# A dynamic 3x3 conv block: far and near parts in place of stacked rows, and fp32 products on two 64x128 tiles

## What is computed

```python
f = relu(einsum('oc,nchw->nohw', Wc, x) + bc)            # 64 channels
gk1 = relu(mean(x, (2, 3)) @ Wc.T + bc)
g_kern = (gk1[:, :, None] * Wkk + bkk).reshape(N, 64, 3, 3)
xm = x.reshape(N, 256, 3, 16, 3, 16).max(axis=(3, 5))
sk = relu(einsum('oc,nckl->nokl', Wc, xm) + bc)
gs = stack([g_kern, sk], axis=2)
dynW = relu(einsum('oj,ncjkl->nockl', Wck, gs) + bck)   # a 3x3 kernel per image and channel pair
y = conv3x3(f, dynW, pad=1) + b_ad                      # each image with its own weights
out = einsum('oc,nchw->nohw', Wf, y) + bf               # back to 256 channels
return x + out
```

## Time and profile before

| | us |
|---|---|
| median of 3 runs | 511.19 (509.42 to 512.63) |
| span of the profiled execution | 507.5 |
| PE busy | 487.8 (96%) |
| ACT busy | 426.6 (84%) |
| DVE busy | 418.9 (83%) |
| POOL busy | 296.2 (58%) |

### The profile page before, as it was taken

How to read it: one execution, slowest core, us unless ns; L and a number is a source line. 1 busy time by engine, 2 the same in 40 slices (tenths; PEclk the granted TensorE clock), 3 DMA queues, 4 the chain that set the end, 5 groups by cost and what they waited for, 6 DMA issues and landing times.

```text
span 507.5 us, 19231 instructions
## 1 busy us (share of the span) xinstructions
PE 487.8 (96%) x8349; PEld 383.7 (76%) x8349; DVE 418.9 (83%) x653; ACT 426.6 (84%) x486; POOL 296.2 (58%) x231
## 2 busy tenths in 40 slices
PE   5989999999999999999999999999999999999993
PEld 2454664677788888888888978888887878888781
DVE  6978879988888889888888988888889887888544
ACT  5779999998999999999999899999999989995231
POOL 5224586555577655556775555577655556765543
PEclk9999999999999999999999999999999999999997
DMA  8945778999898998998999999989999998953467
GB/s 335 418 134 201 265 283 289 366 353 349 323 333 334 323 332 340 348 359 293 320 362 333 333 365 343 318 297 360 307 366 334 341 333 298 361 208 145 185 270 296
DMA packets 48868, 158.01 MB, mean 311 GB/s; under 512 B 4752, under 2 KB 15888, under 8 KB 48784
## 3 DMA queue, kind: packets, MB, share of 16 engines
q1 hardware_dynamic: 34096, 93.07, 54.0%
q10 hardware_dynamic: 14688, 63.70, 31.0%
HBM read 75.94 MB, written 75.50 MB: 298 GB/s over the span
## 4 chain that ended last, share of the span: by engine, by line
PE 81%; ACT 2%; DVE 0%; issue 0%; DVEq 0%; ACTq 0%
PE ps L1129 30%; PE ps L1260 23%; PE ps L1228 21%; PE ps L1179 7%; ACT unused L609 1%; DVE X L859 0%; ACT unused L596 0%; ACT f_hi L688 0%; DVEq L153 0%; ACT f L694 0%; ACT Y L586 0%; PE ps L1372 0%; ACT dyn_b L709 0%; ACT dyn_hi L707 0%; ACTq L130 0%
## 5 line engine op out<-in xcount | busy, mean ns | idle before, releaser
L859 DVE SCALAR_TENSOR_TENSOR X<-ps,out_bias,X 128x960 f32<-128x960 f32 (+1 forms) x189 | 185.2, 1008 | 17.1 <-PE ps L1260 16.8
L1260 PE MATMUL ps<-Y,const 64*64 64x480 f32 (+1 forms) x1536 | 165.1, 486 | 0.0
L596 ACT ACTIVATE unused<-X,neg_mean 128x2304 bf16<-128x2304 f32 x60 | 132.0, 2201 | 0.4 <-DVE neg_mean L998 0.4
L512 POOL TENSOR_TENSOR dyn_a<-const,pool_g 128x576 f32<-128x576 f32 x30 | 34.9, 1165 | 163.8 <-DVE pool_g L883 163.8
L609 ACT ACTIVATE unused<-X 128x2304 bf16<-128x2304 f32 x60 | 126.9, 2115 | 0.0
L1228 PE MATMUL ps<-X,wcn_t 64*64 64x384 f32 (+1 forms) x1296 | 115.5, 486 | 0.7 <-issue 0.7
L935 DVE TENSOR_REDUCE feats<-X 128x6 f32<-128x1536 f32 x64 | 111.6, 1744 | 0.0
L1228 PEld LDWEIGHTS ps<-X,wcn_t 64*64 64x64 f32 x1296 | 82.0, 133 | 29.8 <-issue 7.4
L1260 PEld LDWEIGHTS ps<-Y,const 64*64 64x64 f32 x1536 | 78.2, 133 | 7.5 <-issue 2.8
L527 POOL TENSOR_TENSOR f_lo<-f,f_hi 128x1152 f16<-128x1152 f32 x32 | 71.4, 2232 | 19.5 <-ACT f L694 19.5
L1129 PE MATMUL ps<-f_hi,dyn_hi 64*64 64x480 f16 x1152 | 69.0, 365 | 2.5 <-ACT dyn_hi L715 1.1
(11 more groups left out here) (101 smaller groups left out, 541.8 us busy)
## 6 DMA issues: line engine op xcount, KB each, us to landing
X<-x SPq DMA_DIRECT2D x63, 1152.0 KB, 9.5
out<-X ACTq DMA_DIRECT2D x54, 1152.0 KB, 9.7
out<-X SPq DMA_DIRECT2D x7, 1152.0 KB, 8.0
out<-X SPq DMA_DIRECT2D x6, 480.0 KB, 3.5
stack<-f_hi SPq DMA_DIRECT2D x64, 32.5 KB, 2.5
stack<-f_lo SPq DMA_DIRECT2D x64, 32.5 KB, 5.4
X<-x SPq DMA_DIRECT2D x2, 576.0 KB, 7.1
upper<-f_hi SPq DMA_DIRECT2D x32, 32.5 KB, 3.5
```

Source lines behind the costliest of these rows:

```text
L596: nc.scalar.activation(unused[:, t], pixels(u, t), ACT.Square, scale=1.0 / SIDE, bias=neg_mean[:, n % 2, 1:2], accum_out=feats[:, (n + 1) ...
L859: nc.vector.scalar_tensor_tensor(out=out, in0=unit_psum(piece, bank, col), scalar=out_bias[:, t:t + 1], in1=out, op0=ALU.add, op1=ALU.add) ...
L1260: mm = nc.tensor.matmul(ps[rows, bank + q, col:col + width], wft[lanes, t, rows], Y[lanes, n % 2, at:at + width], start=True, stop=True)
```

## The change

The conv has a far and a near part in place of a main and a rest part. Each is made in three terms of nine taps on four 64x64 tiles, from f alone: 7 rows (336 columns) a tile for the far part, in banks 0 and 1, and 5 rows (240 columns) for the near part, in columns 256 on of banks 4 and 5, which the projection and the statistics also use. The tiles `stack` and `upper` and their DMAs are gone; four small DMAs an image bring the one row of f_hi and f_lo on each side of the seam. ACT copies both parts to Y, of which there is one. The projection uses three chunks of 512, 512 and 128 columns on 128x64 tiles throughout. A unit of the far part is two fp32 products of 336 columns on 64x128 tiles, made in one bank pair; the two near units are made in two turns of 240 columns. Units 1, 2, 3 and 5 use banks 6 and 7, units 0 and 4 banks 2 and 3. POOL takes the high weights and the relu from ACT and the Newton steps of the normalisation from DVE; ACT takes the gains. All stores are issued by SP. All orders are new. The core of the diff:

```diff
-CONV_BANKS = (0, 1)
-REST_BANK = 6
+ROWS = (7, 5)
+PART = tuple(rows * SIDE for rows in ROWS)
+FIRST = (((0, 7), (10, 17)), ((14, 19), (0, 5)))
+NEAR_BANK = 4
+NEAR_AT = 256
+CHUNKS = ((0, 512), (512, 512), (1024, 128))
+UNIT_BANKS = (2, 6, 6, 6, 2, 6)
...
@@ PE @@
-            def product(n, k, t, piece, bank, col):
-                at, width, _ = PIECES[piece]
-                for q, h in ((0, 0), (1, 1), (0, 1), (1, 0)):
-                    lanes, rows = (slice(CM * tile, CM * (tile + 1)) for tile in (q, h))
-                    mm = nc.tensor.matmul(ps[rows, bank + q, col:col + width], wft[lanes, t, rows],
-                                          Y[lanes, n % 2, at:at + width],
+            def product(n, k):
+                t, piece = OUT_UNITS[k]
+                at, width = PIECES[piece]
+                bank = unit_bank(n, k)
+                for h in range(2):
+                    lanes = slice(CM * h, CM * (h + 1))
+                    mm = nc.tensor.matmul(ps[:, bank + h, 0:width], wft[lanes, t, :], Y[lanes, at:at + width],
...
+            def conv(n, part, term):
...
+                if term == 0:
+                    pe.wait_ge(f_evac, count(n, 1, 2))
+                    pe.wait_ge(dyn_hi_ready, highs_done(n, 0))
+                    wait(pe, y_done[part], n)
+                    if part == NEAR:
+
+                        pe.wait_ge(halo_hi[n % 2], 32 * (n // 2 + 1))
+                        pe.wait_ge(f_evac, count(min(n + 2, N), 0, 2))
...
+            def units_near(n):
+                if not inside(n):
+                    return
+                pe.wait_ge(y_done[NEAR], count(n, 1))
+                wait_left(pe, n, 0)
+                pe.wait_ge(f_evac, count(min(n + 3, N), 0, 2))
+                wait_left(pe, n, 3)
+                products_near(n)
...
             for i in range(1, N - 1):
-                conv_main(0, i)
...
+                conv(i, FAR, 0)
+                unit(1, i - 1)
+                if i > TURN:
+                    project_f(i + 1)
+                    unit(2, i - 1)
+                    conv(i, FAR, 1)
+                    group_sums(i + 2)
+                    unit(3, i - 1)
+                    conv(i, FAR, 2)
...
+                units_near(i - 1)
+                conv(i, NEAR, 0)
+                conv(i, NEAR, 2 if i < SUMS else 1)
+                conv(i, NEAR, 1 if i < SUMS else 2)
+                unit(0, i)
...
@@ DVE @@
             for i in range(TURN + 1, N - 1):
-                unit(3, i - 2)
                 middle_maxima(0, i + 2)
-                unit(0, i - 1)
+                unit(1, i - 1)
                 outer_maxima(0, i + 2)
-                gains(i + 1)
                 middle_maxima(1, i + 2)
-                unit(1, i - 1)
-                outer_maxima(1, i + 2)
-                unit(4, i - 1)
-                unit(5, i - 1)
                 unit(2, i - 1)
                 variance(i + 2)
                 negate_mean(i + 3)
-                y_rest_out(i)
-                normalise(i + 2)
+                outer_maxima(1, i + 2)
+                unit(3, i - 1)
+                invert(i + 2)
+                unit(4, i - 1)
+                unit(5, i - 1)
+                unit(0, i)
...
@@ ACT @@
+            for i in range(TURN + 1, N):
+                y_out(i - 1, NEAR)
                 features(i + 1)
+                channel_mean(0, i + 3)
+                channel_mean(1, i + 3)
+                f_out(i + 1)
+                deviation(i + 2)
+                square_sum(0, i + 3)
+                y_out(i, FAR)
+                square_sum(1, i + 3)
...
@@ POOL @@
+            def weights_high(n):
...
+                    nc.gpsimd.tensor_scalar(dyn_hi[:, n % 2], dyn_a[:], MOST, 0.0, ALU.min, ALU.max) \
+                        .then_inc(dyn_hi_ready, 1)
+
+            def weights_relu(n):
...
+                    nc.gpsimd.tensor_scalar(dyn_b[:], dyn_a[:], MOST, 0.0, ALU.min, ALU.max).then_inc(dyn_relu, 1)
...
+            for n in range(SUMS, N):
+                weight_sums(n)
+                weights_high(n)
...
+                    projection(n + 1)
+                    weights_relu(n)
+                    weights_low(n)
+                    f_low(n)
@@ SP @@
+            for i in range(1, N - 1):
+                load(i + AHEAD, 0)
+                seam_low(i)
+                load(i + AHEAD, 1)
+                seam_high(i + 1)
+                store(i - 1, 0)
+                store(i - 1, 1)
```

More of the change, by code:

```diff
@@ L302, in highs_done, with unit_bank @@
             return PIECES_OF_SUMS * n + piece + 1 if n < SUMS else PIECES_OF_SUMS * SUMS + n - SUMS + 1
[L304 to L315, removed]
         def aided(n):
             return {N - 2: PENULT_AIDED, N - 1: LAST_AIDED}.get(n, ())
-        def order(n):
-            return range(UNITS) if n >= N - 2 else ORDER
+        def unit_bank(n, k):
+            return {N - 2: PENULT_BANKS, N - 1: LAST_BANKS}.get(n, UNIT_BANKS)[k]
         def made(n, k):
-            if n < N - 2 and k == 4:
-                k = 5
-            return count(n, order(n).index(k) + 1, UNITS)
+            return count(n, k + 1, UNITS)
         def direct(n):
-            return tuple(k for k in order(n) if k not in aided(n))
+            return tuple(k for k in range(UNITS) if k not in aided(n))
         def results(n, k):
@@ L385, in store @@
             def store(n, t):
-                done = [k for k in direct(n) if units(n)[k][0] == t]
-                wait_result(n, done[-1])
-                for k in aided(n):
-                    if units(n)[k][0] == t:
+                for k in range(UNITS):
+                    if OUT_UNITS[k][0] == t:
                         wait_result(n, k)
@@ L698, in f_out @@
                 if inside(n):
+                    gains(n)
                     f_high(n)
                     f_full(n)
[L702 to L709 removed]
             def early_high(n, piece):
@@ L852, in weight_bounds, with unit @@
                 nc.vector.reciprocal(bnd[:, 13:14], bnd[:, 12:13]).then_inc(bounds_ready, 1)
-            def leave(n, k, t, piece, bank, col):
+            def unit(k, n):
+                if not inside(n) or k in aided(n):
+                    return
+                t, piece = OUT_UNITS[k]
                 dve.wait_ge(out_mm, made(n, k))
@@ L1014, in _ @@
             strip_stats(1, 0)
-            gains(0)
+            early_gains(0)
             for piece in range(PIECES_OF_SUMS):
@@ new lines, in _ @@
+            middle_maxima(0, 3)
+            middle_maxima(1, 3)
+            negate_mean(3)
+            unit(3, 0)
+            unit(4, 0)
+            outer_maxima(0, 3)
+            unit(5, 0)
+            outer_maxima(1, 3)
+            unit(0, 1)
+            unit(1, 1)
+            variance(3)
+            middle_maxima(0, 4)
+            invert(3)
+            unit(2, 1)
+            outer_maxima(0, 4)
+            middle_maxima(1, 4)
+            negate_mean(4)
+            unit(3, 1)
@@ new lines, in _ @@
+            outer_maxima(1, 4)
+            unit(4, 1)
+            unit(5, 1)
+            unit(0, 2)
+            unit(1, 2)
+            variance(4)
+            negate_mean(5)
+            middle_maxima(0, 5)
+            invert(4)
+            unit(2, 2)
+            outer_maxima(0, 5)
+            middle_maxima(1, 5)
+            unit(3, 2)
+            outer_maxima(1, 5)
+            variance(5)
+            negate_mean(6)
+            unit(4, 2)
+            invert(5)
+            unit(5, 2)
@@ L1089, in _, with idle_products @@
         def _(pe):
+            def idle_products(times):
+                pe.wait_ge(pads_zero, 3)
+                for _ in range(times):
+                    nc.tensor.matmul(ps[0:CM // 2, 1, 0:10 * SIDE], f_hi[:, 1, 0, 0:CM // 2],
+                                     f_hi[:, 1, 2:12, 0:SIDE], start=True, stop=True)
             def setup():
@@ L1186, in begin_f @@
+                            f[lanes, n % 2, r:r + ROWS[part], LEFT - 1 + dx:LEFT - 1 + dx + SIDE],
+                            start=(term == 0 and tap == 0), stop=(term == order[-1] and tap == TAPS - 1))
+                if term == order[-1]:
+                    mm.then_inc(conv_mm[part], 1)
             def begin_f(n):
```

813 lines of the change are left out of this document (322 added, 491 removed).

## The result

The changed kernel takes 595.61 us (median, 594.06 to 597.20) against 510.31 of the kernel before on the same chip. The ratio is 1.1675 (95% interval 1.1623 to 1.1726). The forecast was 589 in a range of 548 to 607. The profiled execution has a span of 595.4 us against 507.5, so 87.9 us more.

A forecast was written before the change was run, and what follows sets the result against it. PE was taken to bound the kernel, at 14.62 us an image. 27 steady images add 72 us, start, early images and end 2 + 3 + 1: +78 on a 507.5 span, plus 3.7 to the median, 589 us (range 548 to 607).

The forecast's parts named there:

- The columns: PE's products in a steady image: 14.60 us without form changes and waits, the period of before again.
- Changes of form: Ten changes of tile form an image on PE, at 0.20 us each: 2.0 us an image.
- The rival of free changes between 64x64 and 64x128: Only the two row changes at the projection cost: 558 us, chance 0.14.
- the case in which the kernel is not slower: Tiles change form without a drain and DVE's maxima end in time: 509 us, chance 0.10.
- The wait on DVE: PE's near units wait for DVE's unit 3, behind the outer maxima: 0.7 us an image (0.5 to 0.9).
- The steady sum: 27 steady images, each longer by 2.0 + 0.7 - 0.02 us: +72 us, at a period of 17.3.
- POOL: POOL's turn of 14.1 us stays hidden under 17; rival that POOL or queues bound: 618 us, chance 0.10.
- all this costs nothing while PE is the last: Work moved among DVE, ACT, POOL and queues adds no time, covered by the 3 us of period growth.
- The start: Image 0's near conv waits until f of image 1 has left the shared bank 4: +2 us.
- The early images: Images 1 to 3, which took 50.5 us before: +3 us.
- they take 52, and I allow 1.5 of waits: Three early images at 17.3 us each take 52 us, plus 1.5 us of waits.
- The end: Nine form changes (1.8 us), less 0.8 for units starting during the last near conv: +1 us.

The follow-up runs named there:

- The last run: The kernel of run 9 with its big loads and stores cut to a few columns, same number of DMAs and waits: 523.98 us, ratio 1.0239.
- run 4: The kernel before with its units on two 64x128 tiles instead of four 64x64 ones, nothing else: 544.51 us, ratio 1.0669.
- run 5: The kernel before with its projection of images 5 on made on 128x64 tiles instead of 64x64 ones: 515.81 us, ratio 1.0115.
- run 3: The changed kernel with units on 64x64 tiles and DVE's unit 3 ahead of the outer maxima: 550.98 us, ratio 1.0776.
- run 2: The changed kernel with DVE's unit 3 moved ahead of the outer maxima: 570.34 us, ratio 1.1178.
- run 7: The changed kernel with 15 idle products on PE ahead of image 0's near conv: 595.91 us, ratio 1.1682.
- run 6: The changed kernel with ACT's orders for images 3 and 4 changed so that f leaves PSUM earlier, in two attempts: 599.16 us and 594.78 us.
- run 9: The changed kernel with unit 3 ahead of the maxima, ACT's second early orders, idle products, and every steady product on 64x64 tiles: 553.07 us, ratio 1.0807.

## Why the prediction was right, and where it was off

**The columns.** The working gave 14.60 without changes of form and waits. The last run, with small transfers, measures 14.69 for it in most images, and the run with full ones has 14.69 and 14.78 among its shortest periods. The step held: the far and near split costs about 0.1 us an image and gives nothing.

**Changes of form.** The mechanism held: a far unit takes 0.76 where its columns ask 0.57, and a far conv term with a unit behind it 1.43 where they ask 1.30. Four comparisons price one change: 0.16 (run 4, eight), 0.145 (run 5, two), 0.145 (run 3 against run 2, 16.22 to 15.07, eight), and 0.19 (the last run against run 3, 15.07 to 14.69, two; here the chunks of the projection differ as well). All ten together are 16.22 - 14.69 = 1.53. The term was 10 x 0.20 = 2.0 and should have been 10 x 0.15 = 1.5. The price was read off single groups; the length of the whole image was what counted, and in run 5 other groups gave back 0.09. The rule that I cited from the Trainium skill, page "TensorEngine Tiling (Array Packing)", section "Key Properties", agrees with both kinds of change: runs 4 and 5 show a price for the column split and for the row split. That the price is a drain is not shown by any run. The rival of free changes between 64x64 and 64x128 is out, and with it the case in which the kernel is not slower.

**The wait on DVE.** It came out as worked out, in the place named: 0.84 instead of 0.7 in the trace, and 0.9 by the period without it (17.13 to 16.22). The difference follows from the other term: three of PE's changes lie between the statistics and the near units, and at 0.15 each instead of 0.20 PE arrives 0.15 us earlier and waits that much longer. So the errors of the two terms partly cancel by their nature: the sum of both is 2.4 against a forecast of 2.7.

**The steady sum.** 14.62 + 1.5 + 0.9 + 0.1 = 17.1, measured 17.13, forecast 17.3: 65 us instead of 72. (The last three are differences between measured periods, so this checks that nothing is left over, not that each is right.)

**POOL.** Its chain was priced at 1.65 for a tensor_scalar of 576 columns, from a row that did a single maximum. The same op measured 0.74 for the scaling in the changed kernel:

```profile
L455 POOL TENSOR_SCALAR dyn_a<-per_gain,mean_act 128x576 f32<-128x576 f32 x30 | 22.3, 743 | 179.0 <-ACT mean_act L648 179.0
```

POOL was further from bounding than I had said, and no steady wait of PE names it. No wait of PE in the changed kernel names a queue either. But "all this costs nothing while PE is the last" failed for the early images, where PE is not the last: their projections wait 0.85, 1.15 and 1.19 us for the normalised weights, which POOL now makes:

```profile
PE ps L1112 <- POOL wcn_t L507: 3.2, 3, 1.2
```

**The start.** Forecast +2, measured +7.3. The wait was placed right: the near conv began at 39.11, as worked out. Two things failed. The +2 was charged without a working: from 39.1 on, the near conv (2.9) and unit 0 (0.8) still stand ahead of image 1, which puts its start at 42.8, 4.7 later than 38.1, and image 1, with 18.2 us against 17.7, gave nothing back. And after 3.6 idle us the granted clock was 0.50, so the near conv took 5.55 instead of 2.9; run 7 shows this share as 2.6 us in this trace.

**The early images.** Forecast +3, measured +12.6. I had counted the old waits down to 1.5 us for three images and overlooked that the same condition as in image 0, f out of PSUM before the near units, applies to them all, in images 2 and 3 with six passes of ACT over x instead of the steady four. It is the step "they take 52, and I allow 1.5 of waits" that failed. In its place the trace shows 6.2 us of waits for f, the 3.2 us for POOL's weights, and 3.3 us for the lower clock behind the waits, which another execution need not have (run 6). Neither order of ACT in run 6 made image 3 shorter; whether a better one exists is open. The end was +2.8 against +1.

The start and the early images missed 15 us and the end 2 in one direction. The steady sum missed 7 in the other, and the step from the trace's span to the runs' median another 3.5: the forecast added 3.7 for it, and here it is 0.2. What is left is the 6.6 by which 589 falls short of 595.6. The forecast was right in its mechanism: the two steady terms hold, in place and nearly in size. That its total comes so close is in part luck, since misses in both directions meet in it.

## A version that beats both

None was found. With everything from the change kept but its tile forms and orders, the kernel stays at 551 to 553 us against 510, and even with the transfers taken away it is at 524. Its trace shows where: image 1 starts 4.6 us later than before, images 1 to 3 take 10.0 us more, and 27 steady images 2.0 more (14.75 on average against 14.68). What lies between 524 and the 553 of run 9 is the pauses.

## What to carry to other kernels

Where PE's groups already follow each other at the rate of their columns, fewer or wider products give nothing back, and each change of tile form between groups has to be paid. Count the changes per period, and price them by a whole period and not by the groups beside them. When a bank is shared, look at what stands on the releasing engine between the event that it waits for and the release: a single reduction in the wrong place cost 25 us here. Price the first images by themselves. Conditions that the steady state always meets in time are not met in time there, and an idle stretch of PE can be paid a second time by the clock that is granted after it.

## What the runs showed that I had not expected

With 308 to 332 product records an image on PE in 15 to 16 us and the DMA engines about 80% taken, PE pauses 0.3 to 1.8 us for nothing that the profile names, always at the same place in a block of 256 of its records, and the pauses go when the transfers do (DMA share 0.07). The kernel before has 267 records in 14.62 us at 346 GB/s and one such pause (0.7 us, in front of 418.09), so a kernel can sit near such an edge without showing it. Splitting products into more and smaller ones then costs more than their columns say.
